# Second stage of a gated cross-attention block: two context products ahead of the MLP's last input product, and two of their sums ahead of a shift

## The reference, cut to what matters

```
h  = ln(x)
x1 = layer_norm(h + self_attn(h), ln1)              # causal, 512 wide, one head
x2 = layer_norm(x1 + cross_attn(x1, context), ln2)  # 77 keys
y  = x2 + relu(x2 @ fc1_w + fc1_b) @ fc2_w + fc2_b
x  = x + tanh(g_xattn) * layer_norm(y, ln3)
x  = x + tanh(g_ffn) * ffn(ln(x))                   # 512 -> 2048 -> 512, silu, dequantized weights
```

## Time and profile before

| what | value |
|---|---|
| time, median of 3 runs | 1640.89 us (1640.62 to 1645.77) |
| the profiled execution's own time | 1644.92 us |
| its span | 1643.1 us |
| mean granted clock of TensorE | 0.993 |
| TensorE, VectorE, ScalarE, GpSimd busy | 98%, 53%, 35%, 22% |
| a step of the second stage, t = 1 to 5 | 32.09 to 32.11 us |

### The profile page before, as it was taken

The page is one execution under the profiler, slowest core; times in us unless marked ns, Lnnn a source line. Parts: engine busy times, 40 slices in busy tenths (PEclk is TensorE's granted clock), DMA queues, the critical chain, the costliest instruction groups (busy, mean ns, idle before and its releaser), DMA issues.

```text
span 1643.1 us, 20596 instructions
## 1 busy us (share of the span) xinstructions
PE 1609.2 (98%) x7538; PEld 1322.5 (80%) x7538; DVE 874.4 (53%) x1784; ACT 572.8 (35%) x990; POOL 366.7 (22%) x562
## 2 busy tenths in 40 slices
PE   8999999999999999899999899999999999999999
PEld 6888888877888887677777688888888888888887
DVE  6757444477764435688988966342333332433311
ACT  5432121134222112466566544232323232333322
POOL 1212101022220000388888811000000000000000
PEclk9999999999999999799999999999999999999999
DMA  6302110132121104466655354211212112121100
GB/s 213 100 28 97 45 52 26 39 115 57 60 90 39 39 26 165 118 149 160 172 160 173 103 164 119 64 39 58 45 51 52 52 44 60 39 65 33 46 0 26
DMA packets 177161, 130.87 MB, mean 80 GB/s; under 512 B 121073, under 2 KB 121073, under 8 KB 176907
## 3 DMA queue, kind: packets, MB, share of 16 engines
q1 hardware_dynamic: 175264, 126.10, 26.2%
q10 hardware_dynamic: 1797, 3.46, 0.6%
HBM read 87.34 MB, written 42.18 MB: 79 GB/s over the span
## 4 chain that ended last, share of the span: by engine, by line
PE 84%; DVE 6%; ACT 4%; issue 2%; POOL 2%; DMA 1%; SPq 0%; DVEq 0%; ACTq 0%; POOLq 0%
PE banks L760 81%; PE banks L970 2%; ACT plain L1318 2%; DVE split L1697 1%; ACT split L1154 1%; PE banks L770 1%; DVE plain L2068 1%; ACT plain L1328 1%; DMA tile_x<-x_scratch 1%; DVE plain L2058 1%; DVE tile_x L2075 1%; DMA plain<-in_L_xattn_Wk 0%; ACT plain L1281 0%; POOL split L1572 0%; DVE plain L1836 0%
## 5 line engine op out<-in xcount | busy, mean ns | idle before, releaser
L760 PE MATMUL banks<-split_q,split 128*128 128x512 f32 x2328 | 565.6, 393 | 4.7 <-POOL split L1572 2.7
L760 PE MATMUL banks<-split 128*128 128x512 f32 (+5 forms) x2304 | 542.6, 385 | 6.1 <-DVE split L1697 3.6
L760 PEld LDWEIGHTS banks<-split_q,split 128*128 128x128 f32 x2328 | 434.1, 188 | 98.3 <-POOL split L1572 3.9
L760 PEld LDWEIGHTS banks<-split 128*128 128x128 f32 (+3 forms) x2304 | 414.7, 185 | 101.0 <-DVE plain L1836 7.0
L760 PE MATMUL banks<-split,split_q 128*128 128x512 f32 (+3 forms) x1728 | 392.8, 380 | 4.4 <-DVE split L1697 1.8
L760 PEld LDWEIGHTS banks<-split,split_q 128*128 128x128 f32 x1728 | 308.3, 189 | 57.2 <-DVE split L1697 3.1
L2216 DVE TENSOR_TENSOR split<-plain,split 128x512 fp32r<-128x512 f32 x128 | 88.5, 692 | 387.0 <-ACT split L1473 387.0
L1467 ACT ACTIVATE plain<-banks,small 128x512 f32<-128x512 f32 x128 | 88.3, 690 | 402.7 <-PE banks L760 402.7
L1697 DVE TENSOR_TENSOR split<-banks,split 128x512 fp32r<-128x512 f32 (+5 forms) x232 | 146.1, 637 | 146.4 <-ACT split L1154 146.0
L1154 ACT ACTIVATE split<-banks 128x512 fp32r<-128x512 f32 (+5 forms) x232 | 124.1, 555 | 244.7 <-PE banks L970 190.6
L1506 POOL TENSOR_TENSOR small<-small 128x1 f32<-128x1 f32 x64 | 12.6, 198 | 470.5 <-DVE small L1733 470.3
(11 more groups left out here) (157 smaller groups left out, 1266.3 us busy)
## 6 DMA issues: line engine op xcount, KB each, us to landing
plain<-in_x SPq DMA_DIRECT2D x64, 256.0 KB, 2.7
xo_scratch<-plain SPq DMA_DIRECT2D x32, 256.0 KB, 2.3
x_scratch<-plain SPq DMA_DIRECT2D x32, 256.0 KB, 2.0
plain<-x_scratch SPq DMA_DIRECT2D x32, 256.0 KB, 3.0
tile_x<-xo_scratch SPq DMA_DIRECT2D x32, 256.0 KB, 3.2
xg_scratch<-tile_x SPq DMA_DIRECT2D x32, 256.0 KB, 2.0
out<-plain SPq DMA_DIRECT2D x32, 256.0 KB, 2.1
plain<-xg_scratch SPq DMA_DIRECT2D x7, 1024.0 KB, 5.4
```

The costliest lines, as they stand in the source:

```text
L760: mm = nc.tensor.matmul(out, left(c, l), right(c, r), start=start and c == 0 and (l, r) == PASSES[0], stop=stop and c == chunks - 1 and (l ...
```

## The change

In steps 1 to 6 TensorE issues context products 0 and 1 of tile t + 1 between `mlp_in(t,2)` and `mlp_in(t,3)`; products 2 and 3 stay behind `mlp_in(t,3)`. On VectorE the sums `add_z(t+1,0)` and `(t+1,1)` go between `scale_y(t-1,3)` and `shift_y(t-1,3)`; the other two stay behind the shift. No instruction is added or removed, and the order of ScalarE, GpSimd and SP is the same.

```diff
@@ TensorE, step2(t)
                 if t:
                     mlp_in(t, 2)
+                pair = 2 if ahead and t else 0
+                for k in range(pair):
+                    cross_values(t + 1, k)
                 mlp_in(t, 3)
                 if ahead:
-                    for k in range(BT):
+                    for k in range(pair, BT):
                         cross_values(t + 1, k)
@@ VectorE, step2(t, kept)
                 if t:
                     at = scale_y(t - 1, 3)
+                    add_z(t + 1, 0)
+                    add_z(t + 1, 1)
                     shift_y(t - 1, 3, at)
-                for k in range(BT):
+                for k in range(2 if t else 0, BT):
                     add_z(t + 1, k)
```

## The result

| | before | after |
|---|---|---|
| time, median | 1643.01 us (5 runs, 1640.62 to 1645.77) | 1654.49 us (5 runs, 1653.23 to 1655.88) |
| profiled execution: span, mean granted clock | 1643.1 us, 0.993 | 1654.1 us, 0.991 |

The ratio is 1.0067 with an interval of 1.0053 to 1.0082: slower by more than the 0.3% that can be told, by 11.5 us where 4.0 were forecast. The forecast was built on 1640.89, the median of three runs; the median of all five is 2.1 higher. Against the forecast time of 1644.9 the kernel after is 9.6 above. The time lies outside the range; the direction of the sum was right, its size was not.

A forecast was written before the change was run, and what follows sets the result against it. TensorE is busy 98%, but a loop over TensorE, VectorE and ScalarE was taken to set the period. 5 x 0.8 + 0 for step 6 = +4.0 us on 1640.89 gave 1644.9 us, range 1640.5 to 1648.5.

The forecast's parts named there:

- +0.8 a step: Steps 1 to 5 of the second stage each 0.8 us longer, the later of VectorE's and ScalarE's routes; bounds 0.6 and 1.3.
- The place: Price counted five times in the like steps 1 to 5; step 6 by itself put at nothing, at most 1.3 once.
- TensorE's gap of up to 0.68 goes: TensorE's context products no longer wait for sums, up to 0.68 a step; worth something only if the loop gets shorter.
- ScalarE's route, 0.6 to 0.75: Squares behind relu and hi_hid start about 0.9 later, so ScalarE's hi_x1(4,3) comes 0.6 to 0.75 later.
- The shift ends 1.27 later and the load lands as much later: VectorE's shift_y(1,3) ends at 768.5, +1.27; SP's x1 load behind its store, hence add_z(3,3), starts at 771.7.
- the case in the middle: Shift held until GpSimd's second lo_hid ends, then some 0.6, ending at 768.5 (+1.27), between +0.8 and +1.75.
- VectorE's route makes it 1.27 - 0.45 = 0.8 later.: VectorE's lo_x1(4,3) comes 0.8 later: the fourth sum's 1.27 less 0.45 it stood idle for ScalarE before.
- The granted clock stays at 1.00 in the five steps.: TensorE's clock in steps 1 to 5 stays at 1.00 despite the longer gap; a fall to half would reach rival 1's size.
- rival 1: Shift held for its full 1.67, load lands 1.75 later, each step costs 1.3: 6.5, 1647.4 us; chance 0.20.
- The gap it had forecast: TensorE's idle time before the turns grows from about 0.55 to about 1.9 us.
- Rivals 2 and 3: 2: closed TensorE gap kept, 3.0 less, 1637.9, chance 0.12; 3: late squares and early TensorE cancel, 1640.9, chance 0.16.

The follow-up runs named there:

- e1: TensorE's part of the change alone, VectorE in the order of the kernel before; 1646.69 us against 1642.59, ratio 1.0021.
- e3: The whole change without the load of x1's block 3 from tile 2 on, sum 3 not waiting for it; 1648.95 us, ratio 1.0030.
- e8: TensorE's part, VectorE as before, ScalarE's squares 0 and 1 ahead of relu(t,3); 1650.17 us, ratio 1.0052.
- e11: TensorE's part, VectorE as before, hi_x1(t+2,0) and (t+2,1) ahead of relu(t,3), GpSimd's lo_w(2t) ahead of the fourth root_z; 1644.62 us, ratio 1.0022.
- e6: The whole change with GpSimd's bias_x2(t,2) behind root_y(t,0) instead of ahead of it; 1650.87 us, ratio 1.0048.
- e5: The whole change plus nine unread matmuls before the first turn_x2 in steps 1 to 5; 1650.80 us, ratio 1.0054.
- e4: The whole change with VectorE's scale_w(2t+1) between sums 2 and 3 instead of behind the last transpose; 1649.80 us, ratio 1.0042.
- e12: The changed kernel itself timed and profiled again, to compare with the filled gap on one chip; 1654.71 us, ratio 1.0076.
- e2: VectorE's part of the change alone, TensorE in the order of the kernel before; 1667.25 us, ratio 1.0143.
- e7: TensorE's part, VectorE's scale_y and shift_y ahead of two transposes with all sums behind, squares 0 and 1 ahead of relu(t,3); 1651.41 us, ratio 1.0058.
- e9: The kernel before with ScalarE's hi_x1(t+2,0) ahead of relu(t,3) and hi_x1(t+2,1) behind hi_hid(t,3); 1641.96 us against 1641.33, ratio 1.0007.
- e10: The kernel before with ScalarE's two early hi_x1 copies and GpSimd's lo_w(2t) moved ahead of the fourth root_z; 1639.50 us, ratio 0.9990.
- e13: The whole change plus twelve unread matmuls before the first turn_x2 in steps 1 to 5; 1650.21 us, ratio 1.0051.

## Why the prediction was wrong

The point of the forecast was +0.8 a step; it is +2.77 (+2.53 in the second profile). By its own steps:

- **The place.** Right: the price is in the five copies, step 6 costs 0.5 (forecast 0, at most 1.3), and the chain of waits after passes through the shift, SP, the load and the fourth sum.
- **TensorE's gap of up to 0.68 goes.** Right, and worth nothing, as argued.
- **ScalarE's route, 0.6 to 0.75.** Right: in step 2 the first square starts 0.88 later against `mlp_in(2,2)` and `hi_x1(4,3)` 0.72 later, and e1 and e3, where only this is left, show 32.8 a step, +0.7. What in ScalarE's order would have to move to win it back stays open: squares first (e8) and copies first (e11) both ran into something else.
- **The shift ends 1.27 later and the load lands as much later.** Right. The shift took 1.27 and ended 3.0 behind `scale_y`, as the case in the middle had it; the fourth sum is 1.39 later.
- **"VectorE's route makes it 1.27 - 0.45 = 0.8 later."** This failed. The run from the fourth sum to `lo_x1(t+2,2)` was taken as keeping its length. It got 0.9 longer: the code scaling `scale_w(2t+1)`, 0.67 before, arrives while GpSimd does `bias_x2(t,2)` and lasts 1.55. 1.39 + 0.89 - 0.53 = 1.75, which is what the table has at `add_y`; the 0.53 is what the run from `lo_x1(4,2)` to `add_y(2,0)` got shorter by, 0.45 of it the idle time that the forecast took off. I had used this very holding for the shift and not asked which other instruction with two SBUF sources slides into a GpSimd operation when VectorE is 1.3 late. e6 shows it by moving the addition away: then `add_y` is 0.76 later, which is the forecast's 0.8. The Trainium skill's page "SBUF — State Buffer", section "Who interferes with whom", would have given it: a VectorE instruction with two SBUF inputs contends with a GpSimd instruction that reads SBUF. The rows agree, 0.67 with the addition out of the way and a median of 1.58 beside it.
- **"The granted clock stays at 1.00 in the five steps."** This failed, and is the rest: 34.86 with the falls, 33.86 without (e5), so 1.0 a step in this trace. The last copy, with the long fall, is 1.96 longer than 33.86; the other four are 0.8 longer on average, and so are the five of the second profile. The prediction named it as a way to rival 1's size and gave it no chance of its own. The gap it had forecast was 1.9; at 1.5 to 2.1 e1, e3, e4 and e6 show the clock falling in one to three steps of five, and at 2.8 it fell in every one. So even with the gap that was forecast, a clock that never falls was not to be counted on. The Trainium skill's page "TensorE: Matmul & The Clock Gate", section "HAM oscillation — how this bites in real kernels", describes the same kind of loss: a wait between bursts of matmuls makes each next burst begin at the low clock. The trace agrees as to the kind, with 4.07 for twelve matmuls instead of 3.03. The page has it for longer waits than any here, and its rule would have kept the clock high in these steps; the runs show otherwise, and they decide.
- **Rivals.** Rival 1 (1.3 a step through the load) had the right place and too small a size, and its cause, a shift held for all of its 1.67, did not come: the shift took 1.27. Rivals 2 and 3 fell: TensorE's gain is not kept, and slack was not there.

The sum with measured terms: 1.75 + 1.0 = 2.75 a step, five steps 13.8, step 6 0.5: 14.3. With 0.8 for the clock it is 13.3. The spans differ by 11.0, because the trace before reaches the second stage's step 1 late: `mlp_in(1,0)` starts at 722.54 there and at 719.21 after. That too is TensorE's clock, in a stretch that the change does not touch. From the first `turn_scores` (660.97 and 661.68) to the second, the trace before takes 34.88 at a granted clock of 0.76, and eighteen matmuls in it take 7.52; the trace after takes 30.95 at 0.89, and the same eighteen 4.59. In the other thirteen traces, of whatever version, the stretch takes 30.7 to 32.6 at 0.84 to 0.94. So the profiled execution of the kernel before was an unlucky one there. The medians differ by 11.5, and by 12.3 on the chip of e12, 1 to 2 less than 13.3; how often the clock falls for how long in executions that were not profiled is not known.

## What to carry to other kernels

When an instruction is moved back in a queue, follow what it releases, a transfer above all, to its consumer, and see how much that has in hand; here a load landed 0.02 before the sum that waits for it started. When an engine becomes late, lay its next instructions beside those of the engine that can hold them up (here GpSimd), not only the one that was moved. And add to a longer wait of TensorE what the matmuls behind it cost at the lower clock: here about a third of the loss was that.

## What the runs showed of the hardware

- Work that nobody reads made the kernel faster: 9 or 12 extra matmuls a step, in front of the turns, took away 4 us, because the clock stayed high (1650.21 against 1654.71 on one chip).
- After idle times of TensorE around the turns of 1.54 to 2.07 in all (e1, e3, e4, e6) the clock fell in 8 of 19 steps, after one of 2.53 it did not (the first step of e6), and after 2.80 to 2.95 it fell in ten of ten (the kernel after, profiled twice), as it did in all five steps of e2 after 3.95 to 4.13. In 40 steps with 1.52 or less (the kernel before, e5, e7 to e11, e13) it did not fall. What decides in between stays open.
- The same code scaling of VectorE, with two SBUF sources, took between 0.67 and 1.65, and moving one GpSimd addition brought it back to 0.67 in all five steps. The one that comes second waits: in the kernel before, the scaling started 0.05 ahead of the fourth root's operation on GpSimd and kept its 0.67, and that operation took 1.03 where its like take 0.55. The shift, moved into the middle of a GpSimd operation, took 1.27 instead of 1.67.
